# A gated cross-attention block on one Trainium2 core: the key mask is added by VectorE in its maximum pass, in place of a mask matmul

## The chip, the cores and the metric

The kernel runs on 1 core of one Trainium2 chip. The metric is the device time of one execution in microseconds (us). Each core has five engines with a queue each: TensorE (PE; the rows of its weight loads are called PEld), VectorE (DVE), ScalarE (ACT), GpSimd (POOL) and SyncE (SP, which here only issues DMAs). They meet through semaphores.

## What is computed

Two layers on 4 batches of 256 tokens of width 256, with 512 memory rows of width 128 per batch.

```python
# first layer (one head)
memory_proj = einsum('bme,de->bmd', memory, W_mem)
attn = softmax(einsum('bnd,bmd->bnm', hidden_states, memory_proj) / sqrt(D))
memory_context = einsum('bnm,bmd->bnd', attn, memory_proj)
gate = sigmoid(concatenate([hidden_states, memory_context]) @ W_gate + b_gate)
x = rmsnorm(hidden_states + gate * memory_context, norm_w)
# second layer (16 heads of 64)
q = layernorm(x, ln_q_g, ln_q_b) @ Wq * scale;  k, v = split(media @ Wkv)
sim = where(media_mask, q @ k.T, float32 min)      # media_mask: one bit per batch and memory row
x = x + tanh(attn_gate) * (softmax(sim) @ v) @ Wo
h = layernorm(x, ln_ff_g, ln_ff_b)
x = x + tanh(ff_gate) * gelu(h @ W1) @ W2
```

The mask keeps only the memory rows past a batch's valid length. All of them lie in the last 128 of the 512, and the kernel tests for that at run time. If it holds, the second layer works on 128 keys per batch (the "short" plan, `nt == 1`), otherwise on all 512. In the profile the short plan runs.

## The kernel before

The order of all work is written out by hand: a list of stages for the start (`PROLOGUE`), a generator `body` for the four batches (with the tables `STEADY`, `LAST_BUT_ONE` and `LAST` that place the side work) and a list `TAIL` for the end. Every engine walks the same list and issues its own part of each stage, so the list is at once the order of each engine's queue. Nothing is moved by a scheduler.

In the body a **unit** is 4 heads of one batch, so there are 4 units per batch and 16 in all. A unit's scores are two tiles (n and n+1) of 128 rows by 512 columns, in the two PSUM banks `SC[0]` and `SC[1]`. Each tile holds four blocks of 128 x 128: two token tiles by two heads, the odd heads in one bank and the even ones in the other. This is what the change calls row halves: queries and keys of a head lie in one half of the 128 partitions, and the matmuls of the two halves run side by side. A unit goes through these steps:

- `scores`, TensorE (L1038, L1050): wait until `exp` of the two tiles before is done, one matmul per bank that writes the mask into all four blocks, then eight matmuls q by k that accumulate onto it.
- `scores`, VectorE (L784): one `tensor_reduce` per tile gives minus the row maximum of each of the four blocks (`neg_max`).
- `exp`, ScalarE (L585): four `activation` instructions per tile, from PSUM to `expd` in SBUF, each with the row sum as a second result.
- `norm`: VectorE takes the reciprocals (L792), GpSimd multiplies (L481, `probs`).
- `spread` of the next step: TensorE transposes `probs` (L1080) and ScalarE and VectorE copy the two tiles out (L594, L797). Then `av` (L1171) multiplies with the values, and `wo` (L379, out of `oT_pair`) projects.

`expd` and `probs` are rings of four tiles. Between the scores of a unit and its transposes the list places the output projection of the unit before, `av` of the unit before, and side work: query projections (`q`, L379 out of `xhT_pair`), the first layer of the next batch (`y`, `scores ctx`, `gate`, `fuse`, `rms`), and the layer norms (`x1`, `ln1`, `xhat`, L820, L707, L713). The order of the stages in one unit is:

```python
                if held:
                    yield ("spread", "head", *held)
                yield ("scores", "head", b, u)
                yield ("exp", "head", b, u)
                ...
                yield from first
                yield ("norm", "head", b, u)
                yield from before
```

The mask comes into SBUF as bytes and ScalarE turns it into `mask_bias` (bf16, 0 or -2^100, the same in all 128 partitions; stage `mask`). The mask matmul takes `mask_bias` as the moving tensor and `ones_bf` as weights, a tile with a one in the first row of each half and zeros elsewhere, which GpSimd writes at the start (L460, L468).

## Time and profile before

| what | value |
| --- | --- |
| device time, median of 3 runs (lowest, highest) | 231.01 us (230.68, 231.05) |
| the profiled execution's own time | 232.58 us |
| its span (first to last instruction) | 230.7 us |
| mean granted TensorE clock | 0.993 of full speed |
| busy: PE, DVE, ACT, POOL | 92%, 61%, 55%, 34% of the span |
| start of the 16 units' scores | 41.8, 50.6, 59.7, 66.9; 76.4, 85.3, 94.7, 102.1; 111.6, 122.0, 129.9, 138.1; 148.9, 156.1, 163.3, 171.0 us |
| end of the attention part, start of pure feed-forward | about 183 us |

A row of a timeline gives start and length in us, then engine, line, operation, the tiles and the number of instructions merged into it, and in brackets how long the engine had been idle and who released it. A mean length in ns is that of one instruction with its latency. Two instructions of one engine in a row overlap by a part of it.

### The profile page before, as it was taken

What the parts mean: (1) busy time and instruction counts of PE and PEld (TensorE: products, weight loads), DVE (VectorE), ACT (ScalarE), POOL (GpSimd) and SP (SyncE); (2) the same over time, 40 slices, a digit from 0 to 9 for tenths busy, and PEclk for the clock granted to TensorE, in tenths of its full rate; (3) what the DMA queues carried; (4) which work ended last, traced back from release to release, by engine and by line L of the source; (5) the groups of instructions that cost most, each with busy time, mean ns of one, the idle gap of its engine ahead of it and who ended that gap; (6) DMA issues with size and microseconds to landing.
All of it is one profiled execution on the core that took longest, in us unless ns stands there. A gap on an engine that the chain in (4) does not pass through costs nothing.

```text
span 230.7 us, 4263 instructions
## 1 busy us (share of the span) xinstructions
PE 212.7 (92%) x1520; PEld 170.0 (74%) x1520; DVE 141.8 (61%) x296; ACT 127.4 (55%) x414; POOL 79.5 (34%) x82
## 2 busy tenths in 40 slices
PE   7769997998999999999999977999989999999994
PEld 4546544766976978976989855778867788998993
DVE  1575997635885556985655887867875567125410
ACT  3365754747457646567636466575449775028600
POOL 2030143943175333266331447636373007000000
PEclk9999997999999999999999999999999999999999
DMA  6984005050000000000000000050000000110011
GB/s 203 351 300 149 0 0 182 3 185 0 0 3 0 3 1 1 3 1 0 3 0 4 0 0 0 3 182 0 3 1 3 1 0 4 47 45 0 4 47 53
DMA packets 8463, 10.30 MB, mean 45 GB/s; under 512 B 754, under 2 KB 7668, under 8 KB 8052
## 3 DMA queue, kind: packets, MB, share of 16 engines
q1 hardware_dynamic: 7908, 9.71, 12.3%
q8 instruction: 14, 0.23, 0.4%
q10 hardware_dynamic: 528, 0.26, 0.4%
q14 instruction: 13, 0.11, 0.1%
HBM read 8.92 MB, written 1.05 MB: 43 GB/s over the span
## 4 chain that ended last, share of the span: by engine, by line
PE 56%; issue 13%; DVE 11%; POOL 10%; ACT 9%; POOLq 0%; ACTq 0%; DVEq 0%
PE bank L379 33%; ACT expd L585 6%; POOL probs L481 5%; PE bank L1080 4%; PE bank L1171 4%; PE bank L1050 3%; PE bank L1027 3%; PE bank L1090 3%; DVE neg_max L784 2%; PE bank L1229 2%; POOL wo_pair L519 1%; DVE probsT L797 1%; PE bank L1116 1%; PE bank L1134 1%; PE bank L1126 1%
## 5 line engine op out<-in xcount | busy, mean ns | idle before, releaser
L585 ACT ACTIVATE expd<-bank,neg_max 128x128 f32<-128x128 f32 (+1 forms) x136 | 50.5, 396 | 38.1 <-DVE neg_max L784 38.0
L481 POOL TENSOR_TENSOR probs<-expd,row_rcp 128x512 f32<-128x512 f32 x40 | 42.3, 1069 | 69.8 <-DVE row_rcp L792 63.2
L784 DVE TENSOR_REDUCE neg_max<-bank 128x4 f32<-128x512 f32 (+1 forms) x40 | 25.7, 683 | 6.0 <-PE bank L1050 3.6
L585 ACT ACTIVATION_READ_ACCUMULATOR expd<-bank,neg_max 128x1 f32 x136 | 29.3, 216 | 0.0
L379 PE MATMUL bank<-xhT_pair,wq_pair 128*128 128x256 f32 x192 | 27.5, 293 | 1.1 <-DVE fused L806 1.1
L379 PEld LDWEIGHTS bank<-xhT_pair,wq_pair 128*128 128x128 f32 x192 | 24.6, 194 | 5.0 <-DVE fused L806 1.9
L379 PE MATMUL bank<-wo_pair,oT_pair 128*128 128x256 f32 x192 | 26.6, 288 | 0.0
L1080 PE MATMUL bank<-ident,probs 128*128 128x128 f32 x160 | 22.6, 277 | 3.7 <-POOL probs L481 3.5
L379 PEld LDWEIGHTS bank<-wo_pair,oT_pair 128*128 128x128 f32 x192 | 23.6, 189 | 1.8
L1080 PEld LDWEIGHTS bank<-ident,probs 128*128 128x128 f32 x160 | 17.7, 140 | 8.4 <-POOL probs L481 7.1
L379 PE MATMUL bank<-wq_pair,gelu_pair 128*128 128x256 f32 x192 | 23.2, 281 | 0.4 <-issue 0.3
L379 PEld LDWEIGHTS bank<-wq_pair,gelu_pair 128*128 128x128 f32 x192 | 22.8, 189 | 0.8 <-issue 0.4
L379 PE MATMUL bank<-h2T_pair,w_hi 128*128 128x512 f32 x64 | 20.2, 397 | 0.0
L931 DVE TENSOR_TENSOR gelu_pair<-expd,gelu_pair 128x512 fp32r<-128x512 f32 x16 | 11.0, 692 | 12.0 <-ACT gelu_pair L683 12.0
L792 DVE RECIPROCAL row_rcp<-row_sum 128x4 f32<-128x4 f32 (+1 forms) x40 | 6.2, 169 | 19.3 <-ACT expd L585 19.0
L1050 PEld LDWEIGHTS bank<-k_sb,q_sb 64*128 64x128 f32 x256 | 16.8, 189 | 0.8 <-DVE q_sb L863 0.4
L1171 PE MATMUL bank<-probsT,v_sb 128*64 128x256 f32 x128 | 17.3, 392 | 0.0
L1050 PE MATMUL bank<-k_sb,q_sb 64*128 64x128 f32 x256 | 17.0, 273 | 0.1
L863 DVE COPY q_sb<-bank 128x512 f32<-128x512 f32 x16 | 11.0, 686 | 7.3 <-PE bank L379 7.2
L379 PEld LDWEIGHTS bank<-h2T_pair,w_hi 128*128 128x128 f32 x64 | 11.7, 188 | 3.2 <-issue 0.4
L938 DVE SCALAR_TENSOR_TENSOR x_sb<-bank,gates,x_sb 128x256 f32<-128x256 f32 x8 | 3.9, 484 | 15.5 <-PE bank L379 15.5
L639 ACT CAST oT_pair<-bank 128x512 fp32r<-128x512 f32 x16 | 9.7, 604 | 6.8 <-PE bank L1171 6.6
(125 smaller groups left out, 346.9 us busy)
## 6 DMA issues: line engine op xcount, KB each, us to landing
stage<-in_L_xattn_W_dram SPq DMA_DIRECT2D x2, 1024.0 KB, 5.0
x_sb<-in_x_dram SPq DMA_DIRECT2D x4, 256.0 KB, 8.7
wkv_sb<-in_L_xattn_Wkv_dram SPq DMA_DIRECT2D x1, 1024.0 KB, 9.2
stage<-in_L_xattn_Wq_dram SPq DMA_DIRECT2D x1, 1024.0 KB, 10.3
stage<-in_L_xattn_Wo_dram SPq DMA_DIRECT2D x1, 1024.0 KB, 5.4
out_dram<-x_sb SPq DMA_DIRECT2D x8, 128.0 KB, 1.7
ctx_sb<-in_ctx_dram SPq DMA_DIRECT2D x1, 768.0 KB, 7.1
probs<-in_L_xattn_W_gate_dram SPq DMA_DIRECT2D x1, 512.0 KB, 5.2
```

Of the source, the lines that this page charges most:

```text
L379: last = nc.tensor.matmul(bank_ap, lhs(a), rhs(c), start=start and n == 0, stop=stop and n == 2)
L481: nc.gpsimd.tensor_tensor(probs[:, r, :].rearrange("p (h k) -> p h k", h=hb), expd[:, r, :].rearrange("p (h k) -> p h k", h=hb), row_rcp[: ...
L585: last = nc.scalar.activation(expd[:, r, h * w:(h + 1) * w], SC[n % 2][:, h * w:(h + 1) * w], ACT.Exp, bias=neg_max[:, r, h:h + 1], accum_ ...
L639: nc.scalar.copy(oT_pair[:, HI, (g - 1) % 2, :, :], CONTEXT[:, :].rearrange("p (j n) -> p j n", j=2)).then_inc(act["o"], 1)
L784: nc.vector.tensor_reduce(neg_max[:, r, 0:hb], SC[n % 2][:, :].rearrange("p (h k) -> p h k", h=hb), AX_X, ALU.max, negate=True).then_inc(d ...
L863: nc.vector.tensor_copy(q_sb[:, 2 * j:2 * j + 2, :], path.bank(st)[:, :].rearrange("p (i n) -> p i n", i=2)).then_inc(dve["q"], 1)
L931: nc.vector.tensor_tensor(gelu_pair[:, m, LO, :], expd[:, (c - 1) % RING, :], gelu_pair[:, m, HI, :].bitcast(F32), ALU.subtract).then_inc( ...
L1027: nc.tensor.matmul(SC[n % 2][:, :], yT[:, t * P:(t + 1) * P], ctxT[:, b, :], start=True, stop=True).then_inc(pe["scores"], 1)
L1050: last = nc.tensor.matmul(SC[half][:, at:at + P], q_sb[rows, 2 * u + i, t * P:(t + 1) * P], k_sb[rows, 2 * u + i, b, :], start=False, stop ...
L1080: last = nc.tensor.transpose(SPREAD[n % 2][:, j * P:(j + 1) * P], probs[:, n % RING, j * P:(j + 1) * P], ident[:, :])
L1090: last = nc.tensor.matmul(path.bank(st)[:, 0:N], ctx_sb[:, b * KT + j, :], ctx_probsT[:, j, :], start=j == 0, stop=j == KT - 1)
L1171: last = nc.tensor.matmul(CONTEXT[half * DH:(half + 1) * DH, (h // 2) * N:(h // 2 + 1) * N], v_sb[:, b, head * DH:(head + 1) * DH], probsT ...
```

## The change

VectorE's maximum pass over the row-half scores becomes one fused instruction per head block: `tensor_tensor_reduce` reads the 128 x 128 block from PSUM and the mask from SBUF, adds them, multiplies by -1, writes the result to `expd` in SBUF, and gives the minimum over the row, which is minus the maximum. ScalarE's exponential then works in place in `expd` with scale -1. The mask matmul and `ones_bf` go. TensorE waits before the scores for VectorE's pass of two tiles ago where those were head scores, and for the exponential where they were the first layer's (`ctx`), which keep their old form. VectorE now waits for a free place in the `expd` ring and, once, for the mask.

```diff
@@ Path
+                self.score_kind = [st[1] for st in self.plan if st[0] == "scores" for _ in range(T)]
...
+            def scores_read(self, n):
+
+                return (act["exp"] if self.score_kind[n] == "ctx" else dve["negmax"]), n + 1
@@ gpsimd
-            nc.gpsimd.memset(ones_bf[:, :], 0.0).then_inc(pool_step, 1)
-            gp.wait_ge(pool_step, 2)
+            gp.wait_ge(pool_step, 1)
...
-            gp.wait_ge(rows_cleared, 1)
-            for half in range(2):
-                nc.gpsimd.memset(ones_bf[half * DH:half * DH + 1, :], 1.0).then_inc(const_ready, 1)
@@ scalar, "exp"
-                                last = nc.scalar.activation(
-                                    expd[:, r, h * w:(h + 1) * w], SC[n % 2][:, h * w:(h + 1) * w], ACT.Exp,
-                                    bias=neg_max[:, r, h:h + 1], accum_out=row_sum[:, r, h:h + 1])
+                                here = expd[:, r, h * w:(h + 1) * w]
+                                if st[1] == "ctx":
+                                    last = nc.scalar.activation(
+                                        here, SC[n % 2][:, :], ACT.Exp, bias=neg_max[:, r, h:h + 1],
+                                        accum_out=row_sum[:, r, h:h + 1])
+                                else:
+
+                                    last = nc.scalar.activation(
+                                        here, here, ACT.Exp, bias=neg_max[:, r, h:h + 1], scale=-1.0,
+                                        accum_out=row_sum[:, r, h:h + 1])
@@ vector, "scores"
-                            nc.vector.tensor_reduce(neg_max[:, r, 0:hb],
-                                                    SC[n % 2][:, :].rearrange("p (h k) -> p h k", h=hb),
-                                                    AX_X, ALU.max, negate=True).then_inc(dve["negmax"], 1)
+                            if st[1] == "ctx":
+                                nc.vector.tensor_reduce(neg_max[:, r, 0:1], SC[n % 2][:, :], AX_X, ALU.max,
+                                                        negate=True).then_inc(dve["negmax"], 1)
+                                continue
+
+                            if n >= RING:
+                                ve_.wait_ge(pool["probs"], n - RING + 1)
+                            ve_.wait_ge(act["mask"], 1)
+                            b, w = st[2], BANK // hb
+                            first = b * M + (HOT * P if path.nt == 1 else 0)
+                            for h in range(hb):
+                                last = nc.vector.tensor_tensor_reduce(
+                                    expd[:, r, h * w:(h + 1) * w], SC[n % 2][:, h * w:(h + 1) * w],
+                                    mask_bias[:, first:first + w], -1.0, FAR, ALU.add, ALU.min,
+                                    accum_out=neg_max[:, r, h:h + 1])
+                            last.then_inc(dve["negmax"], 1)
@@ tensor, "scores" with nt == 1
-                            te.wait_ge(act["exp"], first)
-                            te.wait_ge(const_ready, 5)
-                            kept = mask_bias[:, b * M + HOT * P:b * M + (HOT + 1) * P]
-                            bias = kept.rearrange("a (h k) -> a h k", h=1).to_broadcast([P, 4, P])
-                            for half in range(2):
-                                rows = slice(half * DH, (half + 1) * DH)
-                                nc.tensor.matmul(SC[half][:, :].rearrange("p (h k) -> p h k", h=4),
-                                                 ones_bf[rows, :], bias[rows], start=True, stop=False)
+                            for n in (first - 2, first - 1):
+                                te.wait_ge(*path.scores_read(n))
...
-                                            k_sb[rows, 2 * u + i, b, :], start=False, stop=t == T - 1 and i == 1)
+                                            k_sb[rows, 2 * u + i, b, :], start=t == 0 and i == 0,
+                                            stop=t == T - 1 and i == 1)
```

The plan for 512 keys is changed alike; it does not run here.

VectorE's queue around the third unit (59.7 us in the profile), before. L797 copies the transposed probabilities of the unit before, L784 is the maximum pass of the two tiles (`bank3` and `bank4` are `SC`), L820 and L707 are the norm work of the next batch, and L792 the reciprocals that the unit's probabilities wait for.

```order
L797 COPY probsT<-bank6 128x2x2x128
L784 TENSOR_REDUCE neg_max<-bank3 128x4
L784 TENSOR_REDUCE neg_max<-bank4 128x4
L820 SCALAR_TENSOR_TENSOR x_sb<-fused,rms_r,normw_sb 128x256 x2
L707 BN_STATS stats<-x_sb 128x6 x2
L792 RECIPROCAL row_rcp<-row_sum 128x4 x2
L713 BN_AGGR mean_var<-stats 128x2 x2
```

The same place in the changed kernel. L803 is the fused instruction, listed as two: the pass itself and one that writes out its minimum. The pair comes four times per bank.

```order
L818 COPY probsT<-bank6 128x2x2x128
L803 ISA expd,neg_max<-bank3,mask_bias 128x128
L803 ISA neg_max 128x1
...
L803 ISA expd,neg_max<-bank4,mask_bias 128x128
...
L841 SCALAR_TENSOR_TENSOR x_sb<-fused,rms_r,normw_sb 128x256 x2
L715 BN_STATS stats<-x_sb 128x6 x2
L813 RECIPROCAL row_rcp<-row_sum 128x4 x2
```

Two instructions became sixteen; what stands before and behind them is unchanged.

TensorE's queue at the same unit, before: the transposes of the unit before, the two mask matmuls, the eight score matmuls, the output projection, a query projection.

```order
L1080 MATMUL bank<-ident,probs 128x128 x8
L1038 MATMUL bank<-mask_bias,ones_bf 128x512 x2
L1050 MATMUL bank<-k_sb,q_sb 128x128 x8
L379 MATMUL bank<-wo_pair,oT_pair 128x256 x12
L379 MATMUL bank<-xhT_pair,wq_pair 128x256 x12
```

And in the changed kernel:

```order
L1093 MATMUL bank<-ident,probs 128x128 x8
L1065 MATMUL bank<-k_sb,q_sb 128x128 x8
L384 MATMUL bank<-wo_pair,oT_pair 128x256 x12
L384 MATMUL bank<-xhT_pair,wq_pair 128x256 x12
```

Only the two mask matmuls are gone.

## Rows read from the trace of the kernel before

**Rows 1.** The page, first part: busy time, share and instructions of each engine.

```profile
PE 212.7 (92%) x1520; PEld 170.0 (74%) x1520; DVE 141.8 (61%) x296; ACT 127.4 (55%) x414; POOL 79.5 (34%) x82
```

**Rows 2.** Busy time by stretch: PE, PEld, DVE, ACT, POOL, granted clock, DMA share.

```profile
30.00:40.00 10.00, 8.47 (x26) 4.13 (x25) 8.88 (x21) 4.90 (x10) 4.11 (x4) 0.83 0.33 105
75.00:130.00 55.00, 54.62 (x453) 46.05 (x453) 35.89 (x81) 32.30 (x134) 21.07 (x21) 1.00 0.01 2
130.00:178.00 48.00, 42.94 (x359) 33.66 (x358) 35.40 (x76) 29.71 (x118) 26.45 (x24) 1.00 0.07 23
```

**Rows 3.** Who waited for whom, 42 to 180 us: us in total, times, longest.

```profile
ACT expd L585 <- DVE neg_max L784: 36.1, 18, 2.9
PEld bank L1080 <- POOL probs L481: 7.1, 11, 1.7
```

**Rows 4.** Timeline of the fifth unit, 76 to 85 us, all engines.

```profile
76.21 0.21 DVE L792 RECIPROCAL row_rcp<-row_sum 128x1 f32<-128x1 f32 x2
76.37 0.39 PE L1038 MATMUL bank<-mask_bias,ones_bf 64*128 64x512 bf16 x2
76.60 1.05 PE L1050 MATMUL bank<-k_sb,q_sb 64*128 64x128 f32 x16
77.69 1.29 DVE L784 TENSOR_REDUCE neg_max<-bank 128x4 f32<-128x512 f32 x2 [0.52 <-PE bank L1050]
78.41 0.37 ACT L585 ACTIVATE expd<-bank,neg_max 128x128 f32<-128x128 f32 x1 [1.79 <-DVE neg_max L784]
...
82.47 2.04 POOL L481 TENSOR_TENSOR probs<-expd,row_rcp 128x512 f32<-128x512 f32 x2 [3.98 <-DVE row_rcp L792]
84.35 1.04 PE L1080 MATMUL bank<-ident,probs 128*128 128x128 f32 x8
```

**Rows 5.** VectorE's groups by shape: count, busy us, mean ns, idle before.

```profile
L784 DVE TENSOR_REDUCE neg_max<-bank 128x4 f32<-128x512 f32 x32 | 20.5, 682 | 3.7 <-PE bank L1050 3.6
L871 DVE TENSOR_TENSOR oT_pair<-bank,oT_pair 128x512 fp32r<-128x512 f32 x16 | 10.9, 684 | 3.2 <-ACT oT_pair L639 3.2
L804 DVE SCALAR_TENSOR_TENSOR fused<-th,bank 128x256 f32<-128x256 f32 x8 | 3.3, 416 | 0.3
L792 DVE RECIPROCAL row_rcp<-row_sum 128x1 f32<-128x1 f32 x8 | 0.9, 149 | 0.0
```

**Rows 6.** ScalarE's groups by shape, two from PSUM and two from SBUF.

```profile
L683 ACT CAST gelu_pair<-expd 128x512 fp32r<-128x512 f32 x16 | 9.9, 621 | 1.0
L639 ACT CAST oT_pair<-bank 128x512 fp32r<-128x512 f32 x16 | 9.7, 604 | 6.8 <-PE bank L1171 6.6
L599 ACT CAST uT_pair<-bank 128x256 fp32r<-128x256 f32 x4 | 1.5, 372 | 6.6 <-PE bank L1090 6.6
L554 ACT CAST wmem_pair<-wmem_sb 128x256 fp32r<-128x256 f32 x1 | 0.4, 405 | 2.1 <-DMA wmem_sb<-in_L_xattn_W_mem_dram 2.1
```

**Rows 7.** Timeline of the seventh unit, 94.8 to 102 us: a packed stretch of VectorE.

```profile
96.25 1.28 DVE L784 TENSOR_REDUCE neg_max<-bank 128x4 f32<-128x512 f32 x2
...
97.45 0.87 DVE L820 SCALAR_TENSOR_TENSOR x_sb<-fused,rms_r,normw_sb 128x256 f32<-128x256 f32 x2
...
98.36 0.75 DVE L707 BATCH_NORM_STATS2 stats<-x_sb 128x6 f32<-128x256 f32 x2
...
99.14 0.18 DVE L792 RECIPROCAL row_rcp<-row_sum 128x4 f32<-128x4 f32 x1
...
99.40 2.04 POOL L481 TENSOR_TENSOR probs<-expd,row_rcp 128x512 f32<-128x512 f32 x2 [2.89 <-DVE row_rcp L792]
...
101.50 0.65 PE L1080 MATMUL bank<-ident,probs 128*128 128x128 f32 x4 [0.34 <-POOL probs L481]
```

**Rows 8.** Waits of TensorE behind the exponentials, second and last unit; the mask matmul's line.

```profile
57.20 1.70 PE L379 MATMUL bank<-xhT_pair,wq_pair 128*128 128x256 f32 x12 [1.08 <-DVE fused L806]
...
177.40 0.66 PE L1080 MATMUL bank<-ident,probs 128*128 128x128 f32 x4 [0.42 <-POOL probs L481]
...
L1038 PE MATMUL bank<-mask_bias,ones_bf x32: 386/387/387, 41.8 to 171.0; 64*128 64x512 bf16 x32
```

More of the change, by code:

```diff
@@ L29 @@
 MASKED = -(2.0 ** 100)
+FAR = 3.0e38
 RMS_EPS = 1e-6
@@ L186, in gated_attention_block @@
         ones_rows = sb("ones_rows", [P, P])
-        ones_bf = sb("ones_bf", [P, P], BF16)
         mask_u8 = sb("mask_u8", [P, B * M], U8)
@@ L521, in run @@
                                                 ).then_inc(pool["wsplit"], 1)
-            gp.wait_ge(const_ready, 5)
+            gp.wait_ge(const_ready, 3)
             run(paths[1], PRO)
@@ L1022, in run @@
                                 if n >= 2:
-                                    te.wait_ge(act["exp"], n - 1)
+                                    te.wait_ge(*path.scores_read(n - 2))
                                 if t == 0:
@@ L1058, in run @@
                                 n = path.score_no(what, b, u, t)
-                                te.wait_ge(act["exp"], n - 1)
-                                te.wait_ge(const_ready, 5)
-                                nc.tensor.matmul(SC[n % 2][:, :], ones_bf[rows, :],
-                                                 mask_bias[rows, b * M:(b + 1) * M], start=True, stop=False)
+                                te.wait_ge(*path.scores_read(n - 2))
                                 if t == 0:
@@ L1071, in run @@
                                     q_sb[rows, u // 2, t * P:(t + 1) * P],
-                                    k_sb[rows, u // 2, :, :], start=False, stop=True).then_inc(pe["scores"], 1)
+                                    k_sb[rows, u // 2, :, :], start=True, stop=True).then_inc(pe["scores"], 1)
                     elif kind == "spread":
```

## The prediction, made before the changed kernel ran

> **What bounds the kernel now.** I read the totals first: TensorE is busy for 92% of the span, VectorE for 61%, ScalarE for 55% [rows 1]. That would make any matmul removed a gain. The busy time by stretch corrects this [rows 2]. From 75 to 130 us TensorE works 54.62 of 55 us and is the bound. From 130 to 178 us it works 42.94 of 48 while VectorE works 35.40. There TensorE waits about 5 us in sum, and the table of waits says for whom: the transposes L1080 wait 7.1 us for GpSimd's `probs` over 42 to 180 us, and ScalarE's exponentials wait 36.1 us, 18 times, for VectorE's maximum [rows 3]. So two bounds take turns. One is TensorE's own queue. The other is the chain of a unit: scores, maximum, exponentials, reciprocal, `probs`, transposes. The change shortens the first and lengthens the second, so what counts is how often the chain has slack. The timelines tell that unit by unit.
>
> **What it removes.** Each unit loses two mask matmuls. They last 0.39 us each [rows 8], but the two run side by side, and the first score matmul starts 0.23 us after them [rows 4]. So 16 units x 0.22 us = **3.5 us** less on TensorE, all of it on the path wherever TensorE is the bound. GpSimd's memsets of `ones_bf` lie in the first 2.6 us, beside TensorE's warm-up, and are worth nothing. TensorE's new wait, for VectorE's pass in place of the exponentials of two tiles ago, comes earlier than the old one, but the transposes ahead of it in the queue already waited for those exponentials through `probs`. It is worth nothing for head scores, and at most a few tenths in the three `ctx` steps, where `yT` comes behind the same exponentials on ScalarE anyway. VectorE's new wait for the ring asks for the `probs` of two units ago, long done.
>
> **What it adds on VectorE.** Per tile one `tensor_reduce` of 682 ns [rows 5] becomes four passes over 128 columns and four read-outs of one column. No row shows this instruction. The nearest for the pass is a two-source one, PSUM and SBUF: 684 ns at 512 columns (L871) and 416 at 256 (L804) [rows 5], so 1.05 ns a column and 148 ns fixed, and 282 ns at 128. The nearest for the read-out is the smallest instruction, 149 ns (L792, one column) [rows 5]. What counts is start to start. Two reduces of 682 ns take 1.29 us together [rows 4], so the first costs 0.60 and 0.08 is overlap. The pass then costs 0.20. Two small ones of 149 ns take 0.21 us [rows 4], so one costs 0.06.
> - Lower end: 0.20 + 0.06 = 0.26 us a head, if the read-out overlaps the pass as its neighbours do.
> - Upper end: 0.28 + 0.17 = 0.45 us, if nothing overlaps.
> - I take **0.30 us**: the read-out has to wait for part of the pass, but the rows with real overlap are nearer in kind than none at all.
>
> At 0.30 a tile costs 1.2 us instead of 0.60, a unit 2.4 instead of 1.2. The maximum of the first tile comes 0.6 us later, and what stands behind both tiles in VectorE's queue comes 1.2 us later. Busy time grows by at least 16 x 1.2 = 19 us, on 141.8.
>
> **What it changes on ScalarE.** The exponentials read SBUF instead of PSUM. The rows of like shape differ by 17 ns at 512 columns (604 against 621) and by 33 ns at 256 (372 against 405, one instance) [rows 6]. I take 20 ns, so 8 x 0.02 = **0.15 us** a unit, with 0 and 0.26 as ends. ScalarE needs about 0.345 us a head (start to start in the timeline), more than VectorE's 0.30, so it stays the pace within a unit: the last exponential comes 0.6 + 0.15 = **0.75 us** later.
>
> The Trainium skill, VectorE: DVE Perf Modes, in its section on the TRN2 errata, says that ScalarE pays 224 fixed cycles on an SBUF source and 172 on a PSUM one, which at its 1.2 GHz is 43 ns an instruction and 0.35 us a unit. By that the sum below comes out at 241.8 us; the two pairs of rows give 17 and 33 ns, so the trace agrees in sign and shows less.
>
> **Unit by unit.** I followed each of the 16 units through the timeline and asked what TensorE waits for next.
> - *Covered, 2 units* (76.4 and 111.6 us). `probs` ends at 84.5 and its transposes start at 84.35 [rows 4], which looks tight, but its reciprocals had waited behind a query copy and a `ctx` copy on VectorE that TensorE releases. The exponentials were over at 81.1. A delay of 0.75 is hidden. Cost 0.
> - *Behind the exponentials, 9 units* (41.8, 50.6, 66.9, 85.3, 102.1, 148.9, 156.1, 163.3, 171.0). TensorE's next wait hangs on something that ScalarE does behind them. At 50.6 it is the gate: tanh, `fused`, and then L379 waited 1.08 us for it [rows 8]. At 66.9 and 102.1 it is `yT` and the `xhT` copies. At 41.8 it is a value copy. In the last four it is `probs` itself: the second transposes already waited between 0.17 and 0.84 us, in the last unit 0.42 [rows 8]. Cost 9 x 0.75 = 6.7 us.
> - *Packed VectorE, 4 units* (59.7, 94.7, 129.9, 138.1). At 94.7 the reduces (96.25) are followed by L820, L707 and only then, at 99.14, the reciprocal, although the first tile's exponentials were done at about 98.4. GpSimd starts on both tiles at 99.40, and TensorE waits 0.34 us for the second [rows 7]. VectorE's whole 1.2 us goes into the path. Cost 4 x 1.2 = 4.8 us.
> - *The unit at 122.0*: its `probs` have 0.6 us of slack, but the gate chain behind its exponentials sets when VectorE can begin the unit at 129.9. Cost 0.75 us there.
>
> Sum: 6.7 + 4.8 + 0.75 - 3.5 = **+8.8 us**. The profiled execution took 232.58 us, 1.57 above the median of the runs, so it would be 241.4, and the median 231.0 + 8.8 = **239.8 us**. The bounds put through the same sum: with 0.26 a head and nothing on ScalarE, delays of 0.44 and 0.88, +4.4 us, 235.4. If besides half of the cost is hidden by slack that I misread, 231.5.
>
> **The rivals.**
> 1. *VectorE sets the pace of the exponentials.* Above 0.345 us a head ScalarE waits before every head of the second tile. At the full 0.45 the last maximum comes 3.6 us after the start and the last exponential 1.4 later, 5.0 against 3.4 now: 9 x 1.6 + 4 x 2.4 + 1.6 - 3.5 = +22, 253 us. At 0.375 it is about +14, 245. For it: no row shows the instruction, and it leaves a result that the next one reads. Against it: every pair of VectorE instructions in the trace overlaps by 0.08 or more. The skill's same page, in its rules for kernel authors, says to minimise the number of VectorE instructions because each drains its pipe; the trace has 0.08 us of overlap left between two. Chance 0.22.
> 2. *Faster: the chain has the slack and TensorE's 0.22 us a unit is what remains*: 231.0 - 3.5 = 227.5 us. The mechanism is cover by the side work between the scores and the transposes, which TensorE spends 99% busy from 75 to 130 us [rows 2]. It decides where a head costs VectorE no more than 0.17 us, or where the waits I counted have more than 0.75 us behind them. Against it: the 7.1 us of waits for `probs` [rows 3] show that slack is used up in at least seven units. Chance 0.08.
> 3. *Reading SBUF is dearer for ScalarE*, 33 ns each as in the one pair at 256 columns [rows 6]: 0.11 us more in ten units, 240.9 us. This is the case of the skill's rule above. Chance 0.10.
> 4. *Gains and delays cancel*, about 231 us, if most of the nine waits are absorbed one unit on. Chance 0.04.
>
> The forecast keeps 0.56. A difference under about 0.2% (0.5 us) can't be told from none here. Faster 0.08, same 0.04, slower 0.88 (forecast, 1 and 3). The range runs from 233 to 249 us: below it lie rivals 2 and 4, above it the dearer part of rival 1, together about 2 in 10.
>
> **What would show it.** In the changed profile:
> - Pairs at L803: the pass near 280 ns, and start to start 0.30 us a head. 0.45 is rival 1, 0.17 is rival 2.
> - Score matmuls that start right behind the transposes, 0.22 us sooner.
> - VectorE busy for 160 us or more, TensorE less than 92% of the span.
> - From scores to the last exponential 0.75 us longer in a unit; the gap at L820, L707 and the reciprocal of the packed units 1.2 us later.
> - More wait of L1080 for `probs`: 7.1 us before, at least 11 after.
> - Exponentials within 0 to 33 ns of before.
>
> The prediction fails if the fused instruction is far outside 0.26 to 0.45 us a head, since each 0.1 moves the sum by about 7 us, or if the waits pile up so that TensorE's clock falls: it was granted 0.83 of full speed at 30 to 40 us, where it was busy 8.47 of 10 us, and full speed from 130 to 178 at 42.94 of 48 [rows 2]. One such stretch of 10 us would add 1.7 us.

## The result, and the profile after

The changed kernel takes **237.59 us** (median of 4 runs, 237.28 to 238.12) against 230.88 us before: ratio 1.029, 95% interval 1.027 to 1.032. On another chip it came out at 1.030 (1.026 to 1.035). It is 6.7 us slower. The forecast was 8.8 us slower, with 239.8 us as the number and 233 to 249 as the range. The profiled execution took 237.49 us, its span is 235.7 us.

The page, first part:

```profile
PE 210.3 (89%) x1488; PEld 168.1 (71%) x1488; DVE 149.0 (63%) x520; ACT 131.0 (56%) x414; POOL 78.9 (33%) x79
```

Against [rows 1] TensorE is busy 2.4 us less in a longer span. VectorE is busy 7.2 us more and ScalarE 3.6 us more.

Busy time by stretch (PE, PEld, DVE, ACT, POOL, granted clock, DMA share), as in [rows 2]:

```profile
30.00:40.00 10.00, 7.93 (x32) 4.03 (x31) 8.71 (x21) 4.90 (x10) 5.04 (x4) 1.00 0.34 105
...
75.00:130.00 55.00, 53.14 (x433) 45.16 (x433) 37.47 (x162) 33.08 (x130) 20.31 (x21) 1.00 0.01 2
130.00:178.00 48.00, 40.80 (x334) 32.48 (x331) 37.51 (x151) 27.11 (x103) 24.94 (x23) 0.96 0.07 23
```

TensorE now idles where it was full: 53.14 of 55 us against 54.62, and 40.80 of 48 against 42.94. Its clock dips in another place than before (0.96 in the last stretch, full speed at 30 to 40 us), and the mean over the span is 0.993 in both. The dip at 30 to 40 us is why the kernel before starts its body at 41.8 us and this one at 41.0. That it is the dip shows in the half fused kernel of experiment 8, traced twice: its body starts at 41.8 us with the dip and at 41.0 without. The dip differs from one execution to the next, so below I compare medians of runs, and within traces only stretches at full clock, except where it is said.

Who waited for whom, 42 to 185 us, as in [rows 3]:

```profile
ACT expd L593 <- DVE neg_max L803: 37.3, 16, 3.6
...
PEld bank L1093 <- POOL probs L482: 11.8, 14, 2.4
```

The wait of the transposes for `probs` has grown from 7.1 to 11.8 us. ScalarE's wait for the maximum has hardly grown (36.1 to 37.3).

The two new forms on VectorE and the exponential, by shape (count, busy us, mean ns, idle before):

```profile
L593 ACT ACTIVATE expd<-expd,neg_max 128x128 f32<-128x128 f32 x128 | 49.6, 389 | 37.3 <-DVE neg_max L803 37.3
...
L803 DVE CUSTOM_DVE_ANT_0 expd<-bank,mask_bias 128x128 f32<-128x128 f32 x128 | 28.2, 286 | 3.5 <-PE bank L1065 3.4
...
L803 DVE DVE_READ_ACCUMULATOR2_ANT neg_max<- 128x1 f32 x128 | 10.6, 83 | 0.0
```

The seventh unit, the place of [rows 7] (timeline, 92 to 107 us):

```profile
97.33 0.28 DVE L803 CUSTOM_DVE_ANT_0 expd<-bank,mask_bias 128x128 f32<-128x128 f32 x1
97.53 0.29 DVE L803 CUSTOM_DVE_ANT_0 expd<-bank,mask_bias 128x128 f32<-128x128 f32 x1
...
98.29 0.40 ACT L593 ACTIVATE expd<-expd,neg_max 128x128 f32<-128x128 f32 x1 [2.29 <-DVE neg_max L803]
...
98.69 0.39 ACT L593 ACTIVATE expd<-expd,neg_max 128x128 f32<-128x128 f32 x1
...
99.01 0.88 DVE L841 SCALAR_TENSOR_TENSOR x_sb<-fused,rms_r,normw_sb 128x256 f32<-128x256 f32 x2
...
100.97 2.04 POOL L482 TENSOR_TENSOR probs<-expd,row_rcp 128x512 f32<-128x512 f32 x2 [3.39 <-DVE row_rcp L813]
...
101.39 0.56 ACT L546 CAST xT_pair<-bank 128x512 fp32r<-128x512 f32 x1
...
103.06 0.66 PE L1093 MATMUL bank<-ident,probs 128*128 128x128 f32 x4 [0.34 <-POOL probs L482]
```

Read it from the first pass at 97.33:
- The passes follow each other every 0.21 us. The eight of a unit hold VectorE for 1.68 us (to L841 at 99.01) where two reduces held it for 1.20 [rows 7].
- The first exponential starts after 0.96 us. Before it was 0.72 [rows 4].
- The eight exponentials take 3.10 us (98.29 to 101.39), 0.388 a head. Before they took 2.76 us, 0.345 a head.
- `probs` starts after 3.64 us, before after 3.15 [rows 7].

So VectorE's pass was cheaper than forecast, and ScalarE's exponential dearer.

### The profile page after: what moved, and what is told of

Its sections match the earlier page's. It is cut to its first block, busy times and chain, and to the rows that moved or that the text cites. A ratio compares the mean times of both kernels' runs of the same rounds, so it can differ in the third digit from the quotient of the medians.

```text
span 235.7 us, 4452 instructions
## 1 busy us (share of the span) xinstructions
PE 210.3 (89%) x1488; PEld 168.1 (71%) x1488; DVE 149.0 (63%) x520; ACT 131.0 (56%) x414; POOL 78.9 (33%) x79
## 3 DMA queue, kind: packets, MB, share of 16 engines
HBM read 8.92 MB, written 1.05 MB: 42 GB/s over the span
## 4 chain that ended last, share of the span: by engine, by line
PE 49%; DVE 17%; ACT 14%; issue 12%; POOL 5%; DMA 2%; SPq 0%; POOLq 0%; ACTq 0%; DVEq 0%
PE bank L384 29%; ACT expd L593 12%; PE bank L1065 5%; PE bank L1093 4%; PE bank L1103 3%; DVE expd L803 3%; PE bank L1184 3%; PE bank L1048 3%; DMA wmem_sb<-in_L_xattn_W_mem_dram 2%; DVE q_sb L884 1%; DVE oT_pair L892 1%; POOL probs L482 1%; PE bank L1139 1%; POOL xhat L516 1%; POOL xhat L513 1%
## 5 line engine op out<-in xcount | busy, mean ns | idle before, releaser
L593 ACT ACTIVATE expd<-expd,neg_max 128x128 f32<-128x128 f32 x128 | 49.6, 389 | 37.3 <-DVE neg_max L803 37.3
L803 DVE CUSTOM_DVE_ANT_0 expd<-bank,mask_bias 128x128 f32<-128x128 f32 x128 | 28.2, 286 | 3.5 <-PE bank L1065 3.4
L384 PEld LDWEIGHTS bank<-xhT_pair,wq_pair 128*128 128x128 f32 x192 | 24.1, 191 | 5.9 <-DVE fused L827 2.7
L384 PE MATMUL bank<-wo_pair,oT_pair 128*128 128x256 f32 x192 | 27.3, 293 | 0.0
L1093 PEld LDWEIGHTS bank<-ident,probs 128*128 128x128 f32 x160 | 17.7, 140 | 12.2 <-POOL probs L482 11.8
L384 PEld LDWEIGHTS bank<-wo_pair,oT_pair 128*128 128x128 f32 x192 | 24.3, 195 | 1.9 <-issue 0.2
L593 ACT ACTIVATION_READ_ACCUMULATOR expd<-expd,neg_max 128x1 f32 x128 | 24.0, 187 | 0.0
L1065 PE MATMUL bank<-k_sb,q_sb 64*128 64x128 f32 x256 | 19.2, 290 | 1.0 <-DVE q_sb L884 0.7
L1065 PEld LDWEIGHTS bank<-k_sb,q_sb 64*128 64x128 f32 x256 | 16.3, 192 | 4.6 <-issue 4.6
L683 ACT ACTIVATE expd<-bank 128x512 f32<-128x512 f32 x16 | 9.6, 599 | 6.9 <-PE bank L384 5.9
```

What stands on the lines that cost most here:

```text
L384: last = nc.tensor.matmul(bank_ap, lhs(a), rhs(c), start=start and n == 0, stop=stop and n == 2)
L593: last = nc.scalar.activation(here, here, ACT.Exp, bias=neg_max[:, r, h:h + 1], scale=-1.0, accum_out=row_sum[:, r, h:h + 1])
L683: nc.scalar.activation(expd[:, (c - 1) % RING, :], path.bank(st)[:, :], ACT.Gelu).then_inc(act["gelu"], 1)
L803: last = nc.vector.tensor_tensor_reduce(expd[:, r, h * w:(h + 1) * w], SC[n % 2][:, h * w:(h + 1) * w], mask_bias[:, first:first + w], -1. ...
L1065: last = nc.tensor.matmul(SC[half][:, at:at + P], q_sb[rows, 2 * u + i, t * P:(t + 1) * P], k_sb[rows, 2 * u + i, b, :], start=t == 0 and ...
L1093: last = nc.tensor.transpose(SPREAD[n % 2][:, j * P:(j + 1) * P], probs[:, n % RING, j * P:(j + 1) * P], ident[:, :])
```

## The experiments

All ran in five rounds, each beside the kernel before on the same chip. They are told here by subject; experiments 1, 2, 3 and 7 ran first, then 4, 5, 6 and 8, then 9 and the half fused kernel again. The first four take the change apart.

**1. The mask matmul alone out of the kernel before.**

```diff
...
-                            for half in range(2):
-                                rows = slice(half * DH, (half + 1) * DH)
-                                nc.tensor.matmul(SC[half][:, :].rearrange("p (h k) -> p h k", h=4),
-                                                 ones_bf[rows, :], bias[rows], start=True, stop=False)
...
-                                            k_sb[rows, 2 * u + i, b, :], start=False, stop=t == T - 1 and i == 1)
+                                            k_sb[rows, 2 * u + i, b, :], start=t == 0 and i == 0,
+                                            stop=t == T - 1 and i == 1)
```

> The kernel before with the two mask matmuls of each unit taken out and nothing else (the mask is left out of the scores). Theory A, from the trace of the changed kernel: the mask matmul hid the first weight load of the score matmuls, since from the start of the transposes to the output projection TensorE takes 2.18 us with it and 2.06 to 2.13 without; so this gains 16 x 0.05 to 0.12, 0.8 to 1.9 us, about 229.5 us. Rival B, my prediction's term: 0.22 us a unit wherever TensorE is the bound and through the chain elsewhere, 3.5 us, about 227.4 us. The start to start of the first score matmul and the projection tells them apart beside the time.

This kernel leaves out the mask. Measured: ratio 0.998 (0.996 to 1.000), -0.4 us with -1.0 and +0.1 as ends. That lies below theory A's range of 0.8 to 1.9, which only the end of the interval reaches; no gain at all isn't excluded either. Rival B, my own term of 3.5 us, is out. The sixth unit in its timeline:

```profile
83.72 1.16 PE L1043 MATMUL bank<-k_sb,q_sb 64*128 64x128 f32 x16
...
84.81 1.47 PEld L379 LDWEIGHTS bank<-wo_pair,oT_pair 128*128 128x128 f32 x12
```

and the same unit of the kernel before:

```profile
85.31 0.10 PEld L1038 LDWEIGHTS bank<-mask_bias,ones_bf 64*128 64x128 bf16 x2 [0.17 <-issue]
85.32 0.39 PE L1038 MATMUL bank<-mask_bias,ones_bf 64*128 64x512 bf16 x2
85.32 1.08 PEld L1050 LDWEIGHTS bank<-k_sb,q_sb 64*128 64x128 f32 x16
85.54 1.05 PE L1050 MATMUL bank<-k_sb,q_sb 64*128 64x128 f32 x16
86.53 0.41 PEld L379 LDWEIGHTS bank<-wo_pair,oT_pair 128*128 128x128 f32 x3
```

Before, the first weight load of the scores starts with the mask matmul and lies under it, and the whole takes 1.21 us (85.32 to 86.53). Without it nothing lies over the first load, the sixteen score matmuls take 1.16 us instead of 1.05, and the block takes 1.09 us. So 0.22 us of mask matmul saved 0.12 us. That the load is what fills the difference is read from these lines; no run separates it. Nor does every unit gain: by the start of VectorE's pass, five of the fifteen steps from one unit to the next are 0.12 to 0.13 us shorter (those from the units at 41.8, 66.9, 76.4, 102.1 and 111.6 us), the others by 0.07 at most, 0.60 us in all.

**2. VectorE's fused pass alone.** The mask matmul stays and ScalarE reads PSUM.

```diff
-                            nc.vector.tensor_reduce(neg_max[:, r, 0:hb],
-                                                    SC[n % 2][:, :].rearrange("p (h k) -> p h k", h=hb),
-                                                    AX_X, ALU.max, negate=True).then_inc(dve["negmax"], 1)
...
+                            for h in range(hb):
+                                last = nc.vector.tensor_tensor_reduce(
+                                    expd[:, r, h * w:(h + 1) * w], SC[n % 2][:, h * w:(h + 1) * w],
+                                    mask_bias[:, first:first + w], -1.0, 3.0e38, ALU.add, ALU.min,
+                                    accum_out=neg_max[:, r, h:h + 1])
+                            last.then_inc(dve["negmax"], 1)
```

> The kernel before with VectorE's maximum pass alone replaced by the fused instructions; the mask matmul stays (the mask enters the maximum twice) and ScalarE still reads the scores from PSUM. Theory A: a head costs VectorE 0.21 us start to start, a tile 0.85 instead of 0.60, so the first exponential comes 0.24 us later and the work behind the pass 0.48 us later: 9 x 0.24 + 4 x 0.48 + 0.24 = 4.3 us, about 235.2 us. Rival B: VectorE's 7 us of extra busy time are mostly off the path and the loss is on ScalarE, under 2 us, about 232.5 us.

Measured: ratio 1.013 (1.010 to 1.016), +3.0 us, with 2.3 and 3.8 as ends. It lies between theory A (4.3) and rival B (under 2): the pass costs time, but less than theory A's sum. The table of steps behind the experiments shows where that sum was off: the units at 85.3 and 122.0 us pass on nothing and the one at 138.1 passes on half of what I gave it, 3.4 us in fifteen steps. In its trace the body also starts 0.5 us earlier than in the other traces without a dip (40.4 against 40.9 us in experiments 3 and 4), which I did not follow up.

**3. The exponentials from SBUF alone.**

```diff
-                                    expd[:, r, h * w:(h + 1) * w], SC[n % 2][:, h * w:(h + 1) * w], ACT.Exp,
+                                    expd[:, r, h * w:(h + 1) * w],
+                                    SC[n % 2][:, h * w:(h + 1) * w] if st[1] == "ctx"
+                                    else expd[:, r, h * w:(h + 1) * w], ACT.Exp,
```

> The kernel before with one change: the head exponentials read the expd tile in SBUF, in place, instead of the scores in PSUM (they work on what the ring holds, so the scores are left out of the probabilities). Theory A: start to start of a head goes from 0.345 to 0.39 us, the last exponential of a unit comes 0.35 us later, 9 x 0.35 + 0.35, and up to 4 x 0.35 more in the packed units: 3.5 to 4.9 us, about 235 us. Rival B, my prediction's 0.15 us a unit: 1.5 to 2.1 us, about 232.7 us.

This kernel leaves the scores out of the probabilities. Measured: ratio 1.019 (1.016 to 1.021), +4.3 us, in theory A's range. Its groups by shape:

```profile
L585 ACT ACTIVATE expd<-expd,neg_max 128x128 f32<-128x128 f32 x128 | 49.6, 389 | 35.4 <-DVE neg_max L786 35.4
L585 ACT ACTIVATION_READ_ACCUMULATOR expd<-expd,neg_max 128x1 f32 x128 | 23.9, 187 | 0.0
```

and those of the kernel before:

```profile
L585 ACT ACTIVATE expd<-bank,neg_max 128x128 f32<-128x128 f32 x128 | 45.1, 378 | 33.2 <-DVE neg_max L784 33.2
...
L585 ACT ACTIVATION_READ_ACCUMULATOR expd<-bank,neg_max 128x1 f32 x136 | 29.3, 216 | 0.0
```

By the mean lengths, 378 to 389 and 216 to 187 ns, nothing seems to get worse. Start to start a head goes from 0.345 to 0.388 us. The fused pass isn't in this kernel, so the slower exponential is not an effect of VectorE's new pass.

But the slower exponentials are not all of the 4.3 us. In two places, the units at 59.7 and 94.7 us, a small VectorE instruction (`ve`) takes 0.98 us. This is the second of them (timeline, 96 to 107 us):

```profile
100.50 2.09 POOL L481 TENSOR_TENSOR probs<-expd,row_rcp 128x512 f32<-128x512 f32 x2 [2.90 <-DVE row_rcp L794]
...
101.64 0.98 DVE L829 TENSOR_SCALAR ve<-mean_var 128x2 f32<-128x2 f32 x1
```

and the same place in the kernel of experiment 4:

```profile
102.30 0.17 DVE L853 TENSOR_SCALAR ve<-mean_var 128x2 f32<-128x2 f32 x1
```

The `ve` starts 0.1 us into GpSimd's second multiply and ends 0.03 us after it (102.62 and 102.59). In the kernel before the two `ve` of these units take 0.21 and 0.20 us, in the changed kernel 0.17 and 0.18, so they are 1.5 us of this loss and none of the change's. The three parts add up to -0.4 + 3.0 + 4.3 = 6.9 us, against 6.7 for the whole change, but this is in part an accident: without those 1.5 us it would be 5.4. So which of the two, pass or exponentials, is the larger part of the loss is not shown; that both are parts of it is.

**4. The mask matmul put back into the changed kernel.**

```diff
                             for n in (first - 2, first - 1):
                                 te.wait_ge(*path.scores_read(n))
...
+                            for half in range(2):
+                                rows = slice(half * DH, (half + 1) * DH)
+                                nc.tensor.matmul(SC[half][:, :].rearrange("p (h k) -> p h k", h=4),
+                                                 ones_bf[rows, :], bias[rows], start=True, stop=False)
```

> The changed kernel with the mask matmuls put back ahead of the scores (the mask enters twice, with the same result). Theory A: the mask matmul costs TensorE 0.1 us a unit at most, since it hides the first weight loads: 0 to 1.5 us over the changed kernel, 2.9% to 3.5% over before. Rival B, my prediction's 0.22 us a unit: 3.5 us over the changed kernel, 4.4% over before.

Measured: ratio 1.027 (1.024 to 1.030) to the kernel before, beside the changed kernel's 1.030 (1.026 to 1.035) on the same chip. No cost can be seen; rival B's 4.4% is out, and theory A's 2.9% lies in the interval. So what the change saves on TensorE was worth too little to be seen here.

**5. The changed kernel again**, for the comparisons on that chip.

> The changed kernel once more, on the chip of the three others, so that they are compared with it by runs of one chip. Both theories: 2.7% to 3.2% over before.

Measured: 1.030 (1.026 to 1.035), as expected.

**6. The fused pass in place in PSUM.**

```diff
-                                    expd[:, r, h * w:(h + 1) * w], SC[n % 2][:, h * w:(h + 1) * w],
+                                    SC[n % 2][:, h * w:(h + 1) * w], SC[n % 2][:, h * w:(h + 1) * w],
                                     mask_bias[:, first:first + w], -1.0, FAR, ALU.add, ALU.min,
...
-                                        here, here, ACT.Exp, bias=neg_max[:, r, h:h + 1], scale=-1.0,
+                                        here, SC[n % 2][:, h * w:(h + 1) * w], ACT.Exp, bias=neg_max[:, r, h:h + 1], scale=-1.0,
```

> The changed kernel with the fused pass writing back into its PSUM bank and the exponentials reading PSUM as before; TensorE waits for the exponentials again. Theory A: ScalarE's part of the loss goes (4.3 us measured for SBUF reads alone) and VectorE's stays if a pass that writes PSUM costs the same 0.21 us a head: about 3 us over the kernel before. Rival B: writing PSUM costs VectorE more, or the loss is not ScalarE's: 5 us or more over before.

Measured: ratio 1.028 (1.022 to 1.033), +6.4 us. Theory A fails on its condition, a pass that writes PSUM does not cost the same, and rival B holds. Its groups by shape:

```profile
L801 DVE CUSTOM_DVE_ANT_0 bank<-bank,mask_bias 128x128 f32<-128x128 f32 x128 | 32.5, 326 | 3.3 <-PE bank L1063 3.1
...
L801 DVE DVE_READ_ACCUMULATOR2_ANT neg_max<- 128x1 f32 x128 | 17.9, 140 | 0.0
```

The pass takes 326 ns instead of 286, the read-out 140 instead of 83, and start to start a head takes 0.25 us instead of 0.21. In the sixth unit the first exponential starts 1.14 us after the first pass (0.96 in the changed kernel), and its stretch of work on VectorE is 1.96 us instead of 1.69. So VectorE loses most of what ScalarE wins back.

**7. The changed kernel with a signal per head.**

```diff
                                     accum_out=neg_max[:, r, h:h + 1])
-                            last.then_inc(dve["negmax"], 1)
+                                last.then_inc(dve["negmax"], 1)
...
                                 here = expd[:, r, h * w:(h + 1) * w]
+                                sc.wait_ge(dve["negmax"], path.maxima(n, h + 1))
```

> The changed kernel, but VectorE signals after each head's pass instead of after the tile's fourth, and ScalarE waits per head. VectorE's work is the same. Theory A, the chain from scores to the last exponential is the bound: the first exponential starts 0.3 us after the pass begins instead of 0.96, and ScalarE at 0.39 us a head stays behind VectorE's 0.21, so the last one comes 0.63 us earlier, 9 to 10 times: 5.7 to 6.3 us less than the changed kernel, about 231.5 us. Rival B, VectorE's occupancy is the bound (its queue is packed): little changes, 236 us or more.

Measured: ratio 1.005 (1.002 to 1.007), +1.1 us: 5.6 us of the 6.7 are gone although VectorE and ScalarE do exactly the work of the changed kernel. Theory A, nearly to the number; its lower end (5.7) lies within the interval. In most units VectorE's occupancy is not what bounds the kernel; the path from the scores to the last exponential is. What is left of the loss arises in the units at 59.7, 94.7 and 129.9 us, where it is the occupancy (table of steps below).

**8. The fused pass for the first tile only**, with a signal per head. The second tile keeps the mask matmul, the reduce and the exponentials from PSUM.

```diff
...
+                            if not path.fused(n):
+                                nc.vector.tensor_reduce(neg_max[:, r, 0:hb],
+                                                        SC[n % 2][:, :].rearrange("p (h k) -> p h k", h=hb),
+                                                        AX_X, ALU.max, negate=True).then_inc(dve["negmax"], 1)
+                                continue
...
-                            for half in range(2):
+                            for half in (1,):
```

> The fused pass for the first tile of each unit alone, with a signal per head; the second tile in the old form (mask matmul for its bank, one tensor_reduce, exponentials from PSUM). Theory A, from the parts as measured (a fused head 0.21 us, a reduce 0.60, an exponential 0.39 from SBUF and 0.345 from PSUM): the first exponential starts 0.3 us after the pass begins instead of 0.72, the last one ends 3.24 us after it instead of 3.48, VectorE's later work comes 0.25 us later: 10 x -0.24 + 4 x 0.25 = -1.4 us against the kernel before, about 229.5 where before has 230.9. Rival B, VectorE's occupancy decides: no gain or up to 1 us slower than before.

Measured: ratio 0.994 (0.992 to 0.996), and 0.997 (0.994 to 0.999) on another chip: 0.8 to 1.3 us faster than the kernel before. Theory A.

**9. One early head.** The kernel before, but VectorE takes the first head block of the first tile in the fused form and signals it, and then one reduce over the other three.

```diff
-                            nc.vector.tensor_reduce(neg_max[:, r, 0:hb],
-                                                    SC[n % 2][:, :].rearrange("p (h k) -> p h k", h=hb),
+                            skip = 0
+                            if path.early(n):
+                                skip = 1
...
+                                nc.vector.tensor_tensor_reduce(
+                                    expd[:, r, 0:P], SC[n % 2][:, 0:P], mask_bias[:, first:first + P],
+                                    -1.0, 3.0e38, ALU.add, ALU.min,
+                                    accum_out=neg_max[:, r, 0:1]).then_inc(dve["negmax"], 1)
+                            w = BANK // hb
+                            nc.vector.tensor_reduce(neg_max[:, r, skip:hb],
+                                                    SC[n % 2][:, skip * w:].rearrange("p (h k) -> p h k", k=w),
                                                     AX_X, ALU.max, negate=True).then_inc(dve["negmax"], 1)
```

> The kernel before, where VectorE takes only the first head block of a unit's first tile in the fused form (its mask enters twice) and signals it; one tensor_reduce does the other three blocks and one the second tile, as before. ScalarE starts on the first head in SBUF while the reduce runs, and reads the other seven from PSUM. Theory A, the time goes with the stretch from the first maximum pass to the last exponential (10.7 us of time per us of it, and 1.6 per us of VectorE work behind which other work queues, from the runs so far): the stretch falls from 3.49 to about 0.39 + 0.39 + 7 x 0.345 = 3.20 us and VectorE's part grows by 0.1: -0.29 x 10.7 + 0.16 = -2.9 us against the kernel before, about 228 where before has 231. Rival B, with the slack used up other waits take over: -1.4 us or less, no better than the half fused version.

Measured: ratio 0.992 (0.990 to 0.995), -1.8 us: **229.84 us** where the kernel before had 231.59. It is clearly faster than both kernels of the change. The sixth unit in its timeline:

```profile
86.17 0.29 DVE L808 CUSTOM_DVE_ANT_0 expd<-bank,mask_bias 128x128 f32<-128x128 f32 x1 [0.52 <-PE bank L1079]
...
86.39 1.15 DVE L813 TENSOR_REDUCE neg_max<-bank 128x3 f32<-128x384 f32 x2
86.50 0.40 ACT L596 ACTIVATE expd<-expd,neg_max 128x128 f32<-128x128 f32 x1 [1.40 <-DVE neg_max L808]
...
86.98 0.37 ACT L602 ACTIVATE expd<-bank,neg_max 128x128 f32<-128x128 f32 x1
...
89.39 0.42 ACT L623 ACTIVATE th<-bank 128x256 f32<-128x256 f32 x1
```

ScalarE starts 0.33 us after the pass, while the reduce still runs, and is through after 3.22 us. The size expected for the stretch (3.20) is right. The gain expected from it (2.9 us) is not. I had counted ten units. By the starts of VectorE's pass six of the fifteen steps get shorter, by 0.27 us each; those from the units at 66.9, 85.3 and 102.1 us, which grow when the chain gets longer, stay as they were when it gets shorter. What TensorE waits for there instead I did not follow up.

> The half fused version once more, on the chip of the version with one early head. Both theories: 0.6% less than before; Theory A: 0.6% more than the version with one early head.

The second run of the half fused version is the 0.997 above. Between it and the early head lie 0.4%, and the two intervals just overlap (0.990 to 0.995 and 0.994 to 0.999), so that the early head is the faster of the two is likely, not shown.

Side by side: the stretch from the first maximum pass to the end of the eighth exponential in the sixth unit (start of the pass to start of the tanh that follows), VectorE's hold on its queue in the third unit (start of the first pass to start of the norm instruction that writes `x_sb`, which follows at once), and the time against the kernel before (231 us times the ratio less one).

| kernel | stretch, us | VectorE, us | time, us |
| --- | --- | --- | --- |
| before | 3.49 | 1.20 | 0 |
| no mask matmul | 3.49 | 1.20 | -0.4 |
| fused pass alone | 3.73 | 1.69 | +3.0 |
| exponentials from SBUF alone | 3.83 | 1.21 | +4.3 |
| fused, in place in PSUM | 3.89 | 1.96 | +6.4 |
| changed | 4.07 | 1.69 | +6.7, +7.0 |
| changed, mask matmul kept | 4.07 | 1.70 | +6.1 |
| changed, signal per head | 3.50 | 1.70 | +1.1 |
| half fused | 3.32 | 1.45 | -1.3, -0.8 |
| one early head | 3.22 | 1.28 | -1.8 |

The order of the times is that of the stretches, except among kernels whose intervals overlap. The signal per head, which changes the stretch and leaves VectorE's hold, moves the time by 5.6 us. How the stretch and VectorE's hold act together shows in the steps from unit to unit. A step is the time from the start of VectorE's pass in one unit to its start in the next; the table gives how much longer than before it is, in us, by the unit that it starts from. All of it is at full clock, except the value marked with a star, in which the clock dipped.

| kernel | growth to the end of the last row sum | 41.8, 50.6, 138.1, 148.9, 156.1, 163.3 | 66.9, 102.1 | growth of VectorE's hold | 59.7, 94.7, 129.9 | 85.3 | 76.4, 111.6, 122.0 |
| --- | --- | --- | --- | --- | --- | --- | --- |
| fused pass alone | +0.24 | 0.24 to 0.25 | 0.24, 0.25 | +0.49 | 0.49, 0.49, 0.49 | 0.01 | 0.00 |
| exponentials from SBUF alone | +0.28 | 0.27 to 0.29 | 0.27, 0.28 | +0.01 | 1.05, 1.06, 0.05 | 0.06 | 0.00 |
| changed, mask matmul kept | +0.52 | 0.51 to 0.53 | 0.52, 0.53 | +0.50 | 0.49, 0.50, 0.49 | 0.30 | 0.00, 0.00, 0.04 |
| changed, signal per head | -0.05 | -0.16 to 0.02 | -0.03, -0.02 | +0.50 | 0.49, 0.49, 0.96* | 0.03 | -0.12, -0.14, -0.04 |
| one early head | -0.28 | -0.27 to -0.26 | -0.02, -0.01 | +0.08 | 0.08, 0.07, 0.08 | 0.00 | 0.00 |

So there are three kinds of unit. Six, and two more when the chain grows, pass on the growth of the chain to within 0.02 us, counted to the end of ScalarE's last row sum. Three pass on the growth of VectorE's hold. Three pass on next to nothing. The one at 85.3 passes on a part of the largest growth and next to nothing of the smaller ones. The 1.05 and 1.06 are the two places of experiment 3. The kernel with a signal per head also lacks the mask matmul, which alone moves a step by up to 0.13 us (experiment 1).

## Why the prediction was right, and which terms were not

The direction, the mechanism and the range held: VectorE's longer pass and ScalarE's SBUF source lengthen the chain of a unit more than TensorE gains. The number, +8.8 for +6.7 us, is close by luck, because errors of both signs met: with the fused head alone put right (0.21 us), my sum gives +2.3 us, which is below the measured one by more than my forecast is above it.

- **A fused head: I took 0.30 us, measured 0.21**, below my lower end of 0.26. The pass itself was read rightly (282 ns forecast, 286 measured). The step that failed is the read-out: I added it to the pass. It starts together with the next pass, and the pair takes what I had given the pass alone (0.20). Rival 1 (0.45) is out; its point of 0.345 us a head was never near. The first unit of the changed kernel, timeline of VectorE:

```profile
42.16 0.29 DVE L803 CUSTOM_DVE_ANT_0 expd<-bank,mask_bias 128x128 f32<-128x128 f32 x1 [0.51 <-PE bank L1065]
42.37 0.08 DVE L803 DVE_READ_ACCUMULATOR2_ANT neg_max<- 128x1 f32 x1
42.37 0.28 DVE L803 CUSTOM_DVE_ANT_0 expd<-bank,mask_bias 128x128 f32<-128x128 f32 x1
42.58 0.08 DVE L803 DVE_READ_ACCUMULATOR2_ANT neg_max<- 128x1 f32 x1
```

- **An exponential from SBUF: I took 0.02 us more, measured 0.043**, above my upper end of 0.033. This is rival 3, at more than its price, and it holds beside the forecast's mechanism. My rows compared mean lengths of instructions that had no second result, and the loss shows only start to start. To the end of the last row sum it is 0.28 us a unit, 0.035 a head, since the last read-out is shorter from SBUF (0.19 us against 0.24). All my runs from SBUF work in place in `expd`; whether the source or the work in place is what costs is not told apart. The Trainium skill, VectorE: DVE Perf Modes, in its section on the TRN2 errata, gives ScalarE 224 fixed cycles from SBUF and 172 from PSUM, by which I estimate 43 ns; the difference start to start, 0.388 against 0.345 us, agrees with it.
- **The mask matmul: I took 0.22 us a unit, measured 0.12 in the trace and 0.4 us in all.** The step that failed was to read the cost of the mask matmul off the start of the first score matmul behind it. The weight load under it was cover that went with it, and the 0.12 us came through in only five steps of fifteen in experiment 1.
- **The nine units behind the exponentials** were to be late by 0.75 us each. In the kernel of experiment 4, which has the changed pass and exponentials and a trace at full clock, seven of them pass on 0.51 to 0.53 us and the one at 85.3 passes on 0.30; the last has no step behind it. The list was right, the size was 0.52.
- **The packed units** were to be late by 1.2 us each. Those at 59.7, 94.7 and 129.9 pass on 0.49 or 0.50 us, the growth of VectorE's hold, as I had argued; the size was off with that of a fused head. The fourth, at 138.1, was read wrongly: it follows the chain (0.24 with the fused pass alone, -0.27 with the early head).
- **The unit at 122.0** was to cost 0.75 us. It passes on 0.04: the chain of the gate that I gave as the reason doesn't reach the next unit. The two covered units pass on nothing, as forecast.
- With 0.52 for eight units, 0.30 and 0.52 for those at 85.3 and at the end, 0.50 for three packed ones and the measured 0.4 for the mask the sum gives 4.2 + 0.3 + 0.5 + 1.5 - 0.4 = 6.1 us; measured 6.7 (6.3 to 7.3). Where the rest lies is open.
- **Rival 2**, faster, had the right suspicion that the gain on TensorE is real only as cover allows, and is out: the gain is 0.4 us. **Rival 4**, no change, is out by the interval of the ratio (1.027 to 1.032).
- Of the signs to look for, four came: the pass near 280 ns (286), score matmuls 0.22 us sooner behind the transposes (0.97 us against 1.19 in the sixth unit), TensorE below 92% (89%), the wait for `probs` at 11 us or more (11.8). The second of them says little, since the score matmuls then take 0.11 us longer. Five did not come: 0.30 us a head (0.21), VectorE busy for 160 us or more (149.0), the last exponential 0.75 us later (0.58), the reciprocal of the packed units 1.2 us later (0.5), exponentials within 33 ns of before (43 start to start).

## What to carry to other kernels

Before a matmul is removed, look at what runs under it: here its 0.22 us hid a weight load. Where two engines hand tiles on and a third waits for the last of them, the stretch from the first input to the last output decides, and an early signal of the first piece shortens it without less work: the same instructions took 5.6 us less with a signal per head. Sums of parts can agree by accident: look at the steps in the traces before you trust them. Price an instruction start to start in a run of its kind, not by its mean length, above all one with a second result.

## What the runs showed of the hardware that I had not expected

- VectorE's fused pass with a minimum over 128 columns follows itself every 0.21 us into SBUF and every 0.25 us in place in PSUM; its read-out (83 ns, 140 ns beside a PSUM output) starts together with the next pass.
- ScalarE's exponential with a row sum takes 0.345 us a head from PSUM and 0.388 from SBUF (in place) start to start, although the mean lengths differ by 11 ns one way and the read-outs' by 29 ns the other.
- A row of mask matmuls ahead of an accumulation cost 0.4 us in 16 units (between 1.0 and nothing), and none that could be seen in the changed kernel.
- VectorE's `ve`, an instruction of two columns, takes 0.17 us, but where it starts during one of GpSimd's `probs` multiplies it doesn't end before that multiply: it ends 0.02 to 0.03 us after it, at up to 1.04 us long (in the half fused kernel). In the twelve traces this happens 36 times and comes out so 35 times; the other time the multiply ended within the `ve`'s own 0.17 us. In the kernel before it is seen at 136.84 us (0.59 us, to 137.43, the multiply to 137.41).
- TensorE's granted clock dips in some executions to the lower of its two levels, 1.2 GHz, for 3.4 us (36.5 to 39.9 in the kernel before, 140.9 to 144.3 in the changed one, granted 0.50 in both). In averages it shows at 30 to 40 us (0.83, among them the kernel before and the one with an early head) or between 130 and 180 us (0.96 to 0.97, the changed kernel and the one with a signal per head), and in other traces not at all up to 180 us.
